# Two-layer graph network on one core: GpSimd's gamma and beta of the first norm wait for the last shift column of the following step

## What is computed

```python
h = jnp.maximum(_layernorm(x, axis=-1), 0.0)
# three layers:
si = x @ attn_w[l, :d]; sj = x @ attn_w[l, d:]
scores = si[:, :, None] + sj[:, None, :] + attn_b[l]
scores = jnp.where(scores >= 0, scores, 0.2 * scores)
attn = jax.nn.softmax(jnp.where(mask, scores, -jnp.inf), axis=-1)
h = layernorm(x + jnp.einsum('bij,bjd->bid', attn, x), g1[l], beta1[l])
ff = jax.nn.gelu(h @ W1[l] + b1[l], approximate=False) @ W2[l] + b2[l]
x = layernorm(h + ff, g2[l], beta2[l])
...
# one graph-attention layer on the result:
Wh = jnp.matmul(h, W)
e = jax.nn.leaky_relu(e_i[:, :, None] + e_j[:, None, :], negative_slope=ALPHA)
attention = jax.nn.softmax(jnp.where(adj == 0, MASK_VAL, e), axis=2)
h_prime = jnp.matmul(attention, Wh)      # then elu
```

## Time and profile before

| | us |
|---|---|
| median of 3 runs | 2412.83 |
| lowest and highest | 2406.16, 2416.46 |
| the profiled execution | 2410.06 |
| its span, first to last instruction | 2408.3 |
| TensorE busy | 2246.6 (93%) |
| VectorE busy | 1896.2 (79%) |
| ScalarE busy | 1572.4 (65%) |
| GpSimd busy | 1130.3 (47%) |

### The profile page before, as it was taken

One profiled execution on the slowest core, in us unless ns is written; L12 is line 12 of the kernel. 1 busy time (PEld: TensorE's weight loads), 2 busy tenths in 40 slices (PEclk: granted clock), 3 DMA queues, 4 the chain that ended last, 5 costly groups with the idle time before them and its releaser, 6 DMA issues.

```text
span 2408.3 us, 41405 instructions
## 1 busy us (share of the span) xinstructions
PE 2246.6 (93%) x14623; PEld 1707.8 (71%) x14623; DVE 1896.2 (79%) x5051; ACT 1572.4 (65%) x2450; POOL 1130.3 (47%) x2120
## 2 busy tenths in 40 slices
PE   5899999998999999999999999999998999999988
PEld 4666776776767777777777767777675777677777
DVE  7777679758788887888888878978868777777875
ACT  5467566666666676676766657776756657666765
POOL 4344346364264543644545544554544445344643
PEclk9899999999999999999999999999999999999999
DMA  6312012011130112200121102111131010011000
GB/s 221 120 44 91 7 57 84 9 55 49 49 115 3 42 49 84 80 20 26 59 91 62 45 6 92 58 58 45 40 110 40 23 45 7 8 40 27 19 23 31
DMA packets 66221, 128.55 MB, mean 53 GB/s; under 512 B 12985, under 2 KB 53213, under 8 KB 62942
## 3 DMA queue, kind: packets, MB, share of 16 engines
q1 hardware_dynamic: 66014, 125.90, 15.6%
HBM read 111.20 MB, written 14.68 MB: 52 GB/s over the span
## 4 chain that ended last, share of the span: by engine, by line
PE 55%; DVE 27%; issue 6%; ACT 5%; POOL 5%; DMA 2%; SPq 0%; DVEq 0%; POOLq 0%; ACTq 0%
PE OB L1654 36%; PE FBB L1654 11%; DVE mj L1251 5%; DVE pw L1275 4%; PE RB L1654 4%; DVE gT L1289 3%; DVE st L1142 3%; PE TH L1654 2%; DVE junk L1193 2%; DMA adjst<-in_adj 1%; ACT nms L922 1%; DVE xc L1169 1%; DVE nm L1300 1%; DVE xc L1156 1%; POOL xc L678 1%
## 5 line engine op out<-in xcount | busy, mean ns | idle before, releaser
L1654 PE MATMUL OB<-xx,pw 128*128 128x257 f32 x4096 | 942.5, 385 | 16.0 <-DVE xc L1169 13.7
L1654 PEld LDWEIGHTS OB<-xx,pw 128*128 128x128 f32 x4096 | 767.5, 191 | 139.6 <-DVE xc L1169 19.6
L1654 PE MATMUL FBB<-hT,wb 128*128 128x512 f16 x2304 | 566.8, 384 | 36.8 <-DVE gT L1289 35.6
L1654 PE MATMUL OB<-wb,gT 128*128 128x256 f16 x4608 | 572.7, 275 | 10.2 <-DVE gT L1289 10.1
L1654 PEld LDWEIGHTS OB<-wb,gT 128*128 128x128 f16 x4608 | 453.1, 99 | 143.8 <-DVE gT L1289 13.9
L651 POOL TENSOR_SCALAR ve<-mv 128x2 f32<-128x2 f32 x256 | 59.5, 233 | 987.9 <-DVE mv L1145 979.7
L894 ACT ACTIVATE FBB<-FBB,wc 128x512 f32<-128x512 f32 x384 | 252.1, 657 | 291.6 <-PE FBB L1654 291.1
L1289 DVE TENSOR_TENSOR gT<-FBB,gT 128x512 f16<-128x512 f32 x384 | 262.6, 684 | 190.4 <-ACT gT L899 189.8
L1654 PEld LDWEIGHTS FBB<-hT,wb 128*128 128x128 f16 x2304 | 215.3, 99 | 246.7 <-DVE gT L1289 43.1
L905 ACT ACTIVATE pw<-pw,sj 128x512 f32<-128x512 f32 x512 | 334.5, 710 | 58.5 <-DVE pw L1275 57.8
L678 POOL TENSOR_TENSOR xc<-xc,gb 128x256 f32<-128x256 f32 x384 | 290.8, 757 | 42.7 <-ACT xc L869 41.9
(11 more groups left out here) (142 smaller groups left out, 2331.7 us busy)
## 6 DMA issues: line engine op xcount, KB each, us to landing
wb<-w_scratch SPq DMA_DIRECT2D x19, 2048.0 KB, 7.9
adjst<-in_adj SPq DMA_DIRECT2D x56, 512.0 KB, 4.2
xx<-in_x SPq DMA_DIRECT2D x16, 512.0 KB, 5.4
nm<-in_L_gnn_W SPq DMA_DIRECT2D x6, 1024.0 KB, 8.4
gb<-in_L_gnn_g SPq DMA_DIRECT2D x48, 128.0 KB, 2.8
adjst<-in_x SPq DMA_DIRECT2D x6, 1024.0 KB, 10.8
out_x<-adjst SPq DMA_DIRECT2D x48, 128.0 KB, 1.7
pw<-in_adj SPq DMA_DIRECT2D x4, 1024.0 KB, 10.4
```

Source lines behind the costliest of these rows:

```text
L1654: return pe.matmul(o, lhsT, rhs, start=first, stop=last)
```

## The change

In fifteen of the 24 feed-forward steps, GpSimd's first multiplication by gamma (tile 0, first norm) waits, beside its old conditions, until `cc_done` has counted the second group of shift columns of step `k + 1`. The condition in the code picks the steps in which the last row maximum of step `k + 1` stands at place 10 or before: 4, 7, 8, 9, 11, 12, 13, 15, 16, 17, 19, 20, 21, 24 and 28.

```diff
                 if kind == LN1:
                     pool.wait_ge(ht_done, 4 * fi(k) + t // 2 + 1)
+                    if t == 0 and k + 1 < STEPS and max((at for at in prep_tables(k)["row"]), default=END) <= 10:
+                        pool.wait_ge(cc_done, 2 * (k + 1) + 2)
                 else:
                     pool.wait_ge(norm_done[kind], n)
                 pool.tensor_tensor(out=v, in0=v, in1=gb[:, 0, :], op=ALU.mult).then_inc(mul_done[kind], 1)
```

## The result

| | before | changed |
|---|---|---|
| median of 22 runs, us | 2410.85 | 2416.69 |
| ratio, with 95% interval | | 1.0028 (1.0022 to 1.0035) |
| span of the profiled execution, us | 2408.3 | 2413.5 |
| VectorE busy in it, us | 1896.2 | 1883.4 |

The account below looks back on a forecast made before the run. The prediction took TensorE, busy 93%, as the bound, so only moves of its idle waits count. 2410.06 + 3.6 (waits) + 3.4 (clock) = 2417 us, 2418 with half the median offset; 8-in-10 range 2407 to 2426 us.

Parts of the forecast that it names:

- The columns: VectorE's shift columns, long only beside GpSimd's gamma or beta, become short; in step 12 `cc` comes 0.9 us earlier.
- The steps 8, 12, 16, 20: Work queued behind gamma on GpSimd makes pair 1 late, delaying TensorE's transposition by 0.9 us each: +3.6 us.
- Step 28: Same delay with four `x1_add` in GpSimd's block and nothing to spare; TensorE's transposition comes later: +1.5 us.
- The steps 9, 13, 17, 21: TensorE's 2.41 us wait hangs on ScalarE, so early columns gain only 0.16 us each: -0.6 us for the four.
- Step 7: Early columns shorten TensorE's 2.36 us wait: -0.9 us; conversions meeting gamma by the skill's rule would leave 0.4 of it.
- Waits in sum: TensorE's waits over the changed steps: 3.6 + 1.5 - 0.6 - 0.9 = +3.6 us.
- The clock: Clock falls behind long TensorE waits, 1.7 us each, (2 + 1 - 1) falls: +3.4 us, bounds -1.7 and +8.5.
- The base and the noise: Profiled execution 2.8 us below the median, half of this offset added; about 0.5% (12 us) taken as distinguishable.
- That the saving goes through: Rival: GpSimd's `nb` of pair 1 comes in time, -6.1 us, 2404 us, 2407 from the median; chance 0.14.
- That the late pair is caught up: Rival: an existing TensorE wait absorbs the delay and the clock falls as often, 2410 to 2413 us; chance 0.12.
- That the change doesn't do what it says: Rival: columns are long for another reason and `cc` is not earlier, +14.8 us, 2425, from the median 2428; chance 0.05.
- That every new wait brings a fall: Rival: clock falls behind all five new waits, +12.1 us, 2422, from the median 2425; chance 0.09.

Follow-up runs that it names:

- fourth experiment: Kernel before, without the new wait, plus two spare GpSimd powers behind gamma and beta of tile 1 in steps 8, 12, 16, 20: 2415.48 us, ratio 1.0019.
- first experiment: The change's new wait only in the steps that prepare another graph (8, 12, 16, 20, 24, 28), against the kernel before: 2419.80 us, ratio 1.004.
- fifth: Kernel before with GpSimd's second residual and pair 1 ahead of gamma in steps 8, 12, 16, 20, 28, no wait for columns: 2407.79 us, ratio 0.9988.
- second experiment: The change's new wait only in steps 4, 7, 9, 11, 13, 15, 17, 19, 21, against the kernel before: 2407.26 us, ratio 0.9986.
- third experiment: The changed kernel, with GpSimd's second residual and pair 1 put ahead of gamma in steps 8, 12, 16, 20, 28: 2401.06 us, ratio 0.996 to before.
- sixth: The third experiment plus gamma of tiles 0 and 4 waiting for shift columns in steps 1, 2, 25, 26, 27: 2396.32 us, ratio 0.994 to before.

## Why the prediction was right, point by point

- **The columns.** Forecast 0.9 us earlier in step 12, measured 1.46 - 0.55 = 0.9; over all steps some 12 us of VectorE's time, measured 12.2.
- **The steps 8, 12, 16, 20.** Forecast +0.9 each from the chain GpSimd, ScalarE, VectorE, TensorE; measured +0.93 in step 16, the one without a fall, and +0.88 for a delay made in another way (fourth experiment). TensorE's waits were to be 0.1 and 2.3 us and are none and 2.38; ScalarE's wait for `nb` was to be 1.6 us and is 1.73. GpSimd took 0.17 us to answer to `cc` (1031.88 to 1032.05), not the 0.1 of my estimate.
- **Step 28.** Forecast +1.5; its waits grew from 1.16 + 1.08 to 3.66, +1.4. To the end of the kernel it is +3.7, falls of the clock included.
- **The steps 9, 13, 17, 21.** Forecast -0.16 each, measured -0.22 in step 21.
- **Step 7.** Forecast -0.9 from the wait of 2.36 us, and it became 1.45. The wait behind it went from 2.50 to 2.23 us too, but that isn't shown to be the change's doing: it hangs on a mask conversion that waits for its input from memory, and with the new wait in step 7 it is 2.23 to 2.25 us in four kernels, without it 2.50 in three and 2.00 in one (fourth experiment). The first two conversions took 1.82 us after and 1.81 before, so gamma's new place cost them nothing, and the loss that I had worked out from the Trainium skill ("SBUF — State Buffer", "Who interferes with whom") didn't come. The rule itself agrees with the trace: in both kernels the first of the two takes 0.68 us, the second, which meets a GpSimd instruction, 1.21 and 1.22 us, and that GpSimd instruction takes 1.12 and 1.02 us in place of 0.72. Where I went wrong was that before, too, one of the two met such an instruction; the change put another one in its place.
- **Waits in sum.** Forecast +3.6; 4 x 0.9 + 1.4 - 4 x 0.2 - 1.0 (all waits of step 7 that are over 0.25 us) gives +3.2.
- **The clock.** Forecast +3.4, from two falls behind the four waits of 2.3 us, one in step 28 and one less in the steps of 2.41. In the profiled execution it was three, one, and three less, and one less in step 7, so at the places named one fall more in place of two, and none with step 7; other falls came in step 23 and in the last steps. The sum over this execution was right in sign and about half as large: 5.2 us longer in all, of which some 2 are left when the waits are taken off, and part of these come from places that the prediction didn't name. Over many executions the term fits better: the granted clock is 0.9854 in the mean of the changed kernel's 22 runs and 0.9867 in the 23 runs of the kernel before that stand beside the first four experiments. The difference, 0.0013 of 2410 us, makes 3 us (an estimate: it takes all the lost clock to lengthen the span, and the clocks on record have three digits). So the size came out, but not by the count that led to it. That count was a guess, and the experiments show that it could be no more: the waits of 2.38 us in steps 8 to 20 were followed by a fall in 6 of 8 cases (changed kernel and first experiment), those of 2.41 us in 8 of 16 (before, first, fourth and fifth), those of 2.31 us in 4 of 16 (changed kernel, second, third and sixth), those of 1.43 us in none of 4.
- **The base and the noise.** The forecast of 2418 us holds 1.4 us for the median of 3 runs; over 22 runs the median before is 2410.85, 0.8 above the profiled execution. So the base that it set out from was 0.6 us too high, and the change itself was forecast at 7.0 us and is 5.8. The prediction took 0.5% for the least that can be told from no change; the interval measured is 0.22 to 0.35%.
- **The rivals.** That the saving goes through is what the third experiment makes of it, by another order. That the late pair is caught up is out: step 16 is longer by as much as its wait grew. That the change doesn't do what it says is out. That every new wait brings a fall is out for the median, though the first experiment, with +9.0 us, comes near it.

What stays open: step 23, in which the changed kernel's TensorE waits 2.95 us for VectorE in place of 2.33 and the half clock lasts 10.2 us in place of 3.4 (+2.2 us). VectorE waits there for input from memory (`xx<-in_x`), and TensorE's wait varied from 2.44 to 3.11 us over the experiments, the spare instructions and the turned orders alike; no run was made for it.

## What to carry to other kernels

Before an instruction is held back, list what is queued behind it on its engine and who waits for that: here gamma had 20 us to spare, but the ninth instruction behind it had 0.6. Here the urgent work put right behind the wait, and the work with time to spare last, turned a loss of 5.8 us into a gain of 9.8, of which 3.6 come with the new order alone. And where tiny VectorE instructions stand on the path, look whether a GpSimd instruction with two inputs runs beside them.

## What the runs showed of the hardware that was not expected

- A VectorE instruction on 128 x 4 numbers takes 0.16 us alone. If it comes up while a GpSimd instruction on 128 x 256 numbers is running, it lasts until that one is over: in the kernel before all 71 that took more than 0.2 us end 0.02 to 0.03 us behind such an instruction, and the longest took 0.74. In the second experiment one met a GpSimd instruction of 1.81 us at the program's start and took 1.73. The GpSimd instruction keeps its 0.73 us. The large VectorE instructions with one input from PSUM (`gT`) take 0.66 to 0.69 us with or without GpSimd beside them. The Trainium skill ("SBUF — State Buffer", "Who interferes with whom") says that a VectorE instruction with two SBUF inputs contends with a GpSimd instruction that reads SBUF, and that one with at most one such input doesn't, outside the two-port modes; both agree with these rows.
- Waits of TensorE of nearly one length (2.31 to 2.41 us), in the same place of the same step, are followed by a stretch at 1.2 GHz in one execution and by none in another: 18 of 40. Each of these falls costs 1.5 to 1.7 us of its step. A fall more or less in one profiled execution is thus not shown to be an effect of an edit, and the step times have to be compared at an equal number of falls.
- ScalarE answers to the semaphore of `cc` after 0.04 us (1031.88 to 1031.92), GpSimd to the same one after 0.17.
